# Four 128x32 column tiles in place of one 128x128 matmul: the projections and MLP products of a macaron transformer block

## What is computed

```python
x = x + 0.5 * ffn(layernorm(x), w_gate, w_up, w_down)
x = x + attn(layernorm(x), Wq, Wk, Wv, Wproj, lq1, lk1, lq2, lk2)
x = x + 0.5 * ffn(layernorm(x), w_gate, w_up, w_down)

# ffn: fp4_linear(x, w) = fp4(x) @ fp4(w).T, blocks of 16; hidden width 704
h = silu(fp4_linear(x, w_gate)) * fp4_linear(x, w_up)
return fp4_linear(h, w_down)

# attn: q, k of 16 half-heads of width 16 (rms-normed, rotated), v of 8 heads of width 32
attn = softmax(causal(q @ k.T / 4))
attn = attn[:, :, 0] - lam * attn[:, :, 1]
out = layernorm(attn @ v) * (1 - LAMBDA_INIT)
return out @ Wproj.T
```

## Time and profile before

| | |
|---|---|
| median of three runs | 2077.24 us |
| the profiled execution, whole | 2080.57 us |
| its span, first to last instruction | 2078.8 us |
| TensorE matmuls (PE) | 1851.7 us busy, 89%, 13634 instructions |
| TensorE loads (PEld) | 781.3 us, 38%, 13634 instructions |
| DVE / ACT / POOL | 1585.7 / 1578.4 / 1394.8 us (76 / 76 / 67%) |
| mean granted TensorE clock | 0.98 |

### The profile page before, as it was taken

One profiled execution on the slowest core, in us unless ns is written; L12 is line 12 of the kernel. 1 busy time (PEld: TensorE's weight loads), 2 busy tenths in 40 slices (PEclk: granted clock), 3 DMA queues, 4 the chain that ended last, 5 costly groups with the idle time before them and its releaser, 6 DMA issues.

```text
span 2078.8 us, 37296 instructions
## 1 busy us (share of the span) xinstructions
PE 1851.7 (89%) x13634; PEld 781.3 (38%) x13634; DVE 1585.7 (76%) x3836; ACT 1578.4 (76%) x2147; POOL 1394.8 (67%) x1503
## 2 busy tenths in 40 slices
PE   1777999999998899999998899999999889999866
PEld 1343444344333434444342434344443333442233
DVE  8899989797646889998755989998876678740375
ACT  3436788968888788777889798867779798789931
POOL 7689888766535788877754788767775767640254
PEclk9899999999999999999999999999999999999988
DMA  4134544235221445433411444433333444320013
GB/s 129 25 63 82 90 83 85 61 62 99 35 47 29 77 86 110 76 66 56 88 29 42 77 76 83 91 59 75 54 69 62 74 74 76 61 50 1 16 29 73
DMA packets 477479, 136.03 MB, mean 65 GB/s; under 512 B 458224, under 2 KB 477040, under 8 KB 477296
## 3 DMA queue, kind: packets, MB, share of 16 engines
q1 hardware_dynamic: 477296, 133.65, 33.6%
HBM read 11.96 MB, written 8.39 MB: 10 GB/s over the span
## 4 chain that ended last, share of the span: by engine, by line
PE 26%; DVE 24%; POOL 16%; ACT 15%; issue 6%; DMA 5%; SPq 1%; POOLq 0%; ACTq 0%; DVEq 0%
ACT probs L1107 12%; PE psum_o L1406 7%; PE psum L1348 7%; POOL h L920 5%; PE psum L1361 4%; PE psum L1387 4%; DMA hT<-h 3%; DVE psum L1134 3%; DVE hq L1203 2%; POOL x L920 2%; PE psum L1372 2%; DVE hq L1208 1%; POOL probs L1009 1%; POOL hq L930 1%; DVE rscale L1138 1%
## 5 line engine op out<-in xcount | busy, mean ns | idle before, releaser
L1107 ACT ACTIVATE probs<-psum 128x1024 f32<-128x1024 f32 (+2 forms) x1152 | 1052.3, 998 | 124.8 <-PE psum L1387 90.4
L1406 PE MATMUL psum_o<-probs,v_sb 128*32 128x512 f32 (+3 forms) x5120 | 562.7, 539 | 13.3 <-POOL probs L1009 9.5
L1348 PE MATMUL psum<-w_gu_T,xT 128*128 128x512 f16 (+1 forms) x2304 | 507.8, 368 | 44.0 <-DVE qscale L1141 14.1
L920 POOL TENSOR_TENSOR h<-hq,qscale 128x704 f16<-128x704 f32 x256 | 362.4, 1433 | 170.5 <-DVE hq L1208 110.4
L1387 PE MATMUL psum<-q_stack,k_stack 64*128 64x512 f16 (+3 forms) x2560 | 368.4, 351 | 59.8 <-ACT probs L1107 46.3
L1348 PEld LDWEIGHTS psum<-w_gu_T,xT 128*128 128x128 f16 x2304 | 213.0, 99 | 317.5 <-issue 52.0
L1361 PE MATMUL psum<-w_down_T,hT 128*128 128x256 f16 x2176 | 269.2, 279 | 40.1 <-DMA hT<-h 21.9
L1009 POOL TENSOR_SCALAR_AFFINE_SELECT probs<-probs 128x512 f32<-128x512 f32 x256 | 175.4, 696 | 186.6 <-ACT probs L1107 185.8
L1387 PEld LDWEIGHTS psum<-q_stack,k_stack 64*128 64x128 f16 x2560 | 95.8, 93 | 437.1 <-ACT probs L1107 308.7
L1361 PEld LDWEIGHTS psum<-w_down_T,hT 128*128 128x128 f16 x2176 | 210.0, 100 | 107.7 <-issue 36.9
L1022 ACT ACTIVATE hq<-psum,tanh_scale 128x512 f32<-128x512 f32 (+1 forms) x256 | 141.6, 556 | 129.4 <-PE psum L1348 126.6
(11 more groups left out here) (121 smaller groups left out, 2218.0 us busy)
## 6 DMA issues: line engine op xcount, KB each, us to landing
xb<-L_attn_x SPq DMA_DIRECT2D x16, 512.0 KB, 4.2
out<-xb SPq DMA_DIRECT2D x16, 512.0 KB, 3.0
xT<-x SPq DMA_TRANSPOSE x128, 3.1
hT<-h SPq DMA_TRANSPOSE x128, 3.5
k_stack<-st SPq DMA_TRANSPOSE x64, 2.8
q_stack<-st SPq DMA_TRANSPOSE x64, 3.3
k_stack<-L_ffn_w_down SPq DMA_DIRECT2D x1, 704.0 KB, 4.0
k_stack<-L_ffn_w_gate SPq DMA_DIRECT2D x1, 512.0 KB, 5.5
```

The costliest lines, as they stand in the source:

```text
L920: return nc.gpsimd.tensor_tensor(by_block(halves(kind, key)[:, n, :]), by_block(buffers(kind, key)[0]), scale.unsqueeze(2).broadcast_to([P ...
L1107: nc.scalar.activation(to, src, ACT.Exp, scale=HD ** -0.5 / QK_SCALE ** 2)\
L1348: last = nc.tensor.matmul(bank(e)[:, 0:hi - lo], xs[:, x, t % 2, k, :], w_gu_T[:, w, k, lo:hi], start=n == 0, stop=n == len(parts) - 1)
L1406: last = nc.tensor.matmul(psum_o[at:at + VD, q0:CHUNK], v_sb[:, kt // NTC % SLOTS * NTC + kt % NTC, 2 * g + u, :], probs[:, s % 3, 2 * u + ...
```

## The change

Every matmul of a full product is issued as four, one for each group of 32 columns of the stationary operand; each writes the 32 output partitions that belong to it and reads the same moving operand. Order, waits, buffers and semaphores are the same; the last of the four tiles of the last matmul raises the semaphore. `scores`, `values` and the transposes are as before. There are 5632 full matmuls (2304 + 2176 + 768 + 384), so 16896 matmuls and as many loads are added.

```diff
+COLUMNS = 32
+        def by_columns(to, stationary, moving, start, stop):
+
+            for i in range(0, P, COLUMNS):
+                last = nc.tensor.matmul(to[i:i + COLUMNS], stationary[:, i:i + COLUMNS], moving, start=start, stop=stop)
+            return last
...
                     for n, (k, x, w) in enumerate(parts):
-                        last = nc.tensor.matmul(bank(e)[:, 0:hi - lo], xs[:, x, t % 2, k, :],
-                                                w_gu_T[:, w, k, lo:hi],
-                                                start=n == 0, stop=n == len(parts) - 1)
+                        last = by_columns(bank(e)[:, 0:hi - lo], xs[:, x, t % 2, k, :], w_gu_T[:, w, k, lo:hi],
+                                          n == 0, n == len(parts) - 1)
                     last.then_inc(full(e)[0], 1)
...
-                        last = nc.tensor.matmul(bank(e)[:, 0:C], hs[0:n, k, :], w_down_T[0:n, w, :],
-                                                start=i == 0, stop=i == len(parts) - 1)
+                        last = by_columns(bank(e)[:, 0:C], hs[0:n, k, :], w_down_T[0:n, w, :],
+                                          i == 0, i == len(parts) - 1)
```

More of the change, by code:

```diff
@@ L1371, in tensor_stages @@
                     for n, (k, x, w) in enumerate(parts):
-                        last = nc.tensor.matmul(bank(e)[:, 0:hi - lo], xs[:, x, t % 2, k, :],
-                                                w_qkv_T[:, w, k, lo:hi], start=n == 0, stop=n == len(parts) - 1)
+                        last = by_columns(bank(e)[:, 0:hi - lo], xs[:, x, t % 2, k, :], w_qkv_T[:, w, k, lo:hi],
+                                          n == 0, n == len(parts) - 1)
                     last.then_inc(full(e)[0], 1)
@@ L1422, in tensor_stages @@
                     for n, (k, x, w) in enumerate(parts):
-                        last = nc.tensor.matmul(bank(e)[:, 0:C], xs[:, x, t % 2, k, :], w_proj_T[:, w, k, :],
-                                                start=n == 0, stop=n == len(parts) - 1)
+                        last = by_columns(bank(e)[:, 0:C], xs[:, x, t % 2, k, :], w_proj_T[:, w, k, :],
+                                          n == 0, n == len(parts) - 1)
                     last.then_inc(full(e)[0], 1)
```

## The result

The changed kernel takes 2092.55 us (median of runs from 2088.03 to 2094.64) beside 2077.7 us for the kernel before in the same series: 14.9 us more, a ratio of 1.007 with a 95% interval of 1.005 to 1.009. The forecast was 2076.2 with a range of 2067 to 2092, so the time lies just above the range, and "slower by over 0.2%" had a chance of 0.3. The profiled execution took 2088.03 us, 7.5 more than that of before (2080.57). That is a light one of its kind: its mean granted clock was 0.984, where the profiled execution of before had 0.980, and over the four executions of the changed kernel time and clock go together (2088.03 at 0.984, 2094.64 at 0.979).

A forecast was written before the change was run, and what follows sets the result against it. TensorE was taken as the fullest engine, 94% busy between 225 and 1950 us. Switches -2.2 x 0.6 plus fetches +0.3 gave -1.0 us: 2079.6 profiled, median 2076.2, own range 2071 to 2081, 8-in-10 range 2067 to 2092.

The forecast's parts named there:

- The fetches: TensorE's instruction queue: 134 more fetches add 0.5% to a DMA share of 0.35, at most 0.5 us, taken as +0.3.
- Groups of four tiles cost what a full matmul takes: Full products on TensorE: four fp16 tiles take 216, 163 and 109 ns for 512, 384 and 256 columns, adding 0.
- issue: Rival, chance 0.09: TensorE's sequencer feeds instructions only every 30 ns, so a group takes 240 ns; 2560 us.
- exposed loads: Rival, chance 0.05: each fp16 group pays 0.026 us for its weight load, 146 us in all; 2215 us.
- tiles in turn: Rival, chance 0.02: four tiles sharing a moving operand run one after another on TensorE, 2.6 ms more.
- The switches: TensorE's stage borders: about 0.10 us per change of array form, some saved and some added, sum -2.2 us.
- How much of TensorE's time arrives: Share of TensorE's saved time reaching the end: 60%, taken between the chain's 26% and TensorE's 94%.
- Latency: Rival, chance 0.13: each full product on the chain hands over 0.035 us later, about 180 stages, +6 us; 2083.
- The signs of being wrong: Forecast is wrong if TensorE's start-to-start distance changes at all or its granted clock over 225 to 1950 us leaves 1.00.
- others: Remaining chance of 0.02 for causes not named among the rivals, counted under slower.

The follow-up runs named there:

- results later: Kernel before, untiled, with each of the 704 full products ended by one more matmul over 60 columns with zero weights: 2087.55 us, ratio 1.0047.
- all six: Changed kernel, tiles in gate and up alone, 64-column tiles, tiles only beside values, unused weight loads, added zero matmuls: +14.9, +7.3, +5.4, +0.3, +16.3, +10.5 us.
- the five experiments: Against the kernel before: tiles in gate and up alone, 64-column tiles, tiles only beside values, unused weight loads, added zero matmuls: +7.3, +5.4, +0.3, +16.3, +10.5 us.
- the run with 512 bytes: Kernel before with a 512-byte transfer issued on SyncE's queue just ahead of every third transposing DMA, 128 in all: 2098.69 us, +21.7.
- Beside values: Kernel before with column tiles only for the 105 runs of full products that stand beside a values stage: 2078.9 us, ratio 1.000.

## Why the prediction failed

The fetches, which were put at +0.3 us, are the step that failed. Step by step:

- *Groups of four tiles cost what a full matmul takes: right.* 109, 163 and 216 ns in the trace. The rivals of issue, exposed loads and tiles in turn, 0.16 together, are gone.
- *The switches: right in kind, too small in size.* 0.10 us gone between values and full products, 0.10 new at the transposes; the sum was -6.9 us where -2.2 was put, since leaving column tiles costs 0.010 us and entering nothing.
- *How much of TensorE's time arrives: put at 60%, by the fit 0.40.* The busy share of 94% was given too much weight against the chain's 26%, which was nearer. On -2.2 or -6.9 us this is an error of a us or two.
- *Latency: the hand-over of 0.02 to 0.035 us is right, 0.025 in the trace; its price is open.* The rival had +6 us; the fit gives 1.5 and does not exclude 6, and "results later" alone bounds it under 10.5.
- *The instruction fetches: this step failed.* "33792 more add 134 fetches and 0.5% to a DMA share of 0.35; the waits for transposed h are 21.9 us, so at most 0.5 us: I take +0.3." The count was right (132), the share too (0.8% for 0.4%). The conclusion was not: it scaled a wait by a mean share, as if the fetches thinned the transfers evenly. A fetch is one packet of 16 KB that takes 1.0 us, a transpose needs all of its packets, and the kernel loses 0.3 us for every us by which a transpose is late. The fit over all six puts the term at 16 us, the five experiments alone at 12. It was bounded from above by a wait (21.9 us) that could itself grow, and did, to 29.5. The trace of before would have given another bound: its 108 fetches had met 88 transposes, 0.8 each. 134 x 0.8 meetings of 0.5 to 1.0 us are 54 to 107 us of later transposes (measured: 78), and at a share of a third (the run with 512 bytes; before it, only "between none and all") 18 to 36 us. Even the low end, put in place of the +0.3, gives a median of 2094 and lies outside the range that was given.
- *The signs of being wrong watched TensorE alone.* Neither came: its distances and the granted clock of 1.00 stayed. None of the named rivals stood for a longer wait at the transfers, so what happened had the 0.02 of "others"; that "slower" had 0.30 was owed to latency and to three rivals that did not come.

The Trainium skill, "Runtime: NRT & Kernel Launch", Instruction fetch mechanics, says that the engines' instructions are refilled in blocks of 256 (16 KiB) over a DMA queue of their own and that the cost of crossing into a new block is mostly hidden. The trace agrees on the block: 33792 instructions more made 132 fetches more, of 16384 bytes each. It is hidden for the engine that fetches, whose distances are unchanged. It is not hidden for the DMAs beside it: by the fits above, 0.09 to 0.12 us of time for each block in this kernel.

## What to carry to other kernels

Count the instructions that a rewrite adds, divide by 256, and ask what transfer a 1 us packet can hold up: in a kernel whose engines wait for short transfers just in time, each block cost some 0.12 us, as much as a switch of the array's form. Tiling four ways multiplies a product's instructions by four. An estimate from the fit: a switch saved gives 0.10 x 0.40 = 0.04 us and an instruction costs 0.122 / 256, so it pays only with fewer than some 85 added instructions for each switch saved. Beside values there were 9162 for 109, 84 each, and that came out level (1.000). Never bound a contention term by the waits that stand there now: a transfer that lands just in time shows no wait, and is the first to show one.

## What the runs showed of the hardware

- A no-op on TensorE takes 71 ns from start to start; an unused whole-array weight load takes 39 ns, is hidden behind a running matmul of 109 ns or more, and stands bare behind a switch (0.12 us for three).
- Four fp16 column tiles with one moving operand run at the pace of the whole matmul down to 256 columns: 8 instructions in 109 ns, in runs of 68 matmuls. Inside a group the tiles start about 5 ns apart, and the result is handed over 0.025 us later.
- A plain transfer of 16 KB within device memory is cut into packets of 1 KB and lands 0.3 us behind one of 512 bytes (2.1 and 1.8 us); an instruction fetch of the same size is one packet of 1.0 us. The 256-byte packets near a fetch take 54 ns in the mean, the others 21.
- 0.50 us of SyncE ahead of one transpose in three costs 20 us of 2077, though SyncE has 1% of the chain in the earlier trace rows: in this kernel the queue that issues the transfers is nearer to the critical path than its share of the chain says.
- Changes between whole array, row halves and column tiles cost 0.093 to 0.116 us each, and tiles of 64 beside tiles of 32 columns are a change like any other (0.11).
